# Feed-forward of a four-layer MetaFormer kernel: first product in one fp32 pass, two of three clips as a minimum on GpSimd

## The reference

```python
def quantize(y):                      # per group g of batch rows (here 5 groups)
    gamma = max(abs(y[g]))            # one number per group
    return clip(y[g] * 128 / (gamma + 1e-5), -128 + 1e-5, 128 - 1e-5)

def bitlinear(x, W, b):
    return quantize(x @ binarize(W).T + b)

h = gelu(bitlinear(layernorm(t), W1, b1))     # 96 -> 384
t = t + bitlinear(h, W2, b2)                  # 384 -> 96
```

## Time and profile before

| | |
|---|---|
| median of 3 runs | 970.29 us (969.41 to 970.37) |
| the profiled execution's own time | 968.89 us |
| its span | 967.0 us |
| busy: TensorE (PE) | 826.8 us, 86% |
| busy: VectorE (DVE) | 617.0 us, 64% |
| busy: GpSimd (POOL) | 560.8 us, 58% |
| busy: ScalarE (ACT) | 436.7 us, 45% |
| granted TensorE clock, mean | 0.918 |
| share of the chain that ended last, by engine | PE 63%, DVE 13%, POOL 8%, issue 8%, ACT 6% |

### The profile page before, as it was taken

The page is one execution under the profiler, slowest core; times in us unless marked ns, Lnnn a source line. Parts: engine busy times, 40 slices in busy tenths (PEclk is TensorE's granted clock), DMA queues, the critical chain, the costliest instruction groups (busy, mean ns, idle before and its releaser), DMA issues.

```text
span 967.0 us, 24067 instructions
## 1 busy us (share of the span) xinstructions
PE 826.8 (86%) x8814; PEld 681.2 (70%) x8814; DVE 617.0 (64%) x1713; ACT 436.7 (45%) x788; POOL 560.8 (58%) x887
## 2 busy tenths in 40 slices
PE   4666767767888999997999899999758998999997
PEld 3555655656666788876887677788757887778886
DVE  5765678637775777673667347677635665476755
ACT  1433345325555444433877354344134554544441
POOL 5333263143433886875776266887615666767855
PEclk9887679669999999997999899999956999999999
DMA  8500010000002101100001000100000001001020
GB/s 177 102 21 0 1 41 1 1 0 2 0 25 66 51 27 38 37 2 1 1 0 43 25 26 26 51 24 27 2 1 1 1 1 50 26 27 50 24 75 18
DMA packets 39512, 26.40 MB, mean 27 GB/s; under 512 B 27464, under 2 KB 32313, under 8 KB 39377
## 3 DMA queue, kind: packets, MB, share of 16 engines
q1 hardware_dynamic: 38428, 24.46, 10.1%
q10 hardware_dynamic: 998, 0.80, 0.3%
HBM read 8.33 MB, written 1.57 MB: 10 GB/s over the span
## 4 chain that ended last, share of the span: by engine, by line
PE 63%; DVE 13%; POOL 8%; issue 8%; ACT 6%; DMA 1%; ACTq 0%; POOLq 0%; DVEq 0%
PE PS L1522 17%; PE PS L1495 7%; PE PS L1496 6%; PE PS L1499 4%; PE PS L1438 3%; PE PS L1581 3%; PE PS L1593 2%; PE PS L1310 2%; ACT H L606 2%; PE PS L1622 2%; PE PS L1603 2%; PE PS L1296 2%; PE PS L1612 2%; PE PS L1357 1%; POOL H L514 1%
## 5 line engine op out<-in xcount | busy, mean ns | idle before, releaser
L648 ACT ACTIVATE H<-PS,B 128x512 f32<-128x512 f32 x288 | 176.9, 685 | 212.1 <-PE PS L1499 211.5
L1522 PE MATMUL PS<-M,H 128*64 128x96 f32 x4608 | 203.8, 249 | 7.2 <-DVE X L1134 7.2
L1522 PEld LDWEIGHTS PS<-M,H 128*64 128x64 f32 x4608 | 194.9, 139 | 18.2 <-DVE X L1134 7.8
L443 POOL TENSOR_TENSOR msum<-stats 128x4 f32<-128x4 f32 (+1 forms) x61 | 15.9, 260 | 277.4 <-DVE stats L808 240.4
L1134 DVE SCALAR_TENSOR_TENSOR X<-PS,G,X 128x96 f32<-128x96 f32 (+1 forms) x384 | 121.0, 317 | 66.3 <-PE PS L1522 55.8
L1496 PE MATMUL PS<-FHL,M1l 128*128 128x512 f32 x192 | 76.7, 400 | 0.0
L1495 PE MATMUL PS<-XH,M1h 128*128 128x512 f32 x192 | 76.6, 399 | 0.0
L487 POOL TENSOR_TENSOR ex<-euler,dl 128x16 f32<-128x16 f32 x24 | 69.8, 2910 | 8.6 <-DVE dl L1098 8.4
L479 POOL TENSOR_TENSOR PF<-G,B 128x1536 f32<-128x1536 f32 x24 | 66.2, 2756 | 10.0 <-DVE G L1125 10.0
L457 POOL TENSOR_TENSOR rs<-ve,half 128x4 f32<-128x4 f32 (+1 forms) x61 | 65.7, 1077 | 4.8
L1310 PE MATMUL PS<-ident,XN 128*96 128x128 f32 x224 | 39.1, 302 | 23.2 <-DMA WM<-L_conv_b_out 12.4
(11 more groups left out here) (250 smaller groups left out, 1928.3 us busy)
## 6 DMA issues: line engine op xcount, KB each, us to landing
FHL<-XH SPq DMA_DIRECT2D x36, 192.0 KB, 2.5
FHL<-XL SPq DMA_DIRECT2D x36, 64.0 KB, 2.2
X<-XH SPq DMA_DIRECT2D x12, 192.0 KB, 2.5
raw<-L_ffn_w SPq DMA_DIRECT2D x3, 576.0 KB, 4.7
M<-L_ffn_w SPq DMA_DIRECT2D x3, 576.0 KB, 6.0
X<-x SPq DMA_DIRECT2D x4, 384.0 KB, 6.2
XH<-XL SPq DMA_DIRECT2D x24, 64.0 KB, 1.9
out<-X SPq DMA_DIRECT2D x8, 192.0 KB, 2.4
```

The source lines that it names most:

```text
L648: act.activation(H[p][:, c, :], bank(UB[c]), ACT.Gelu, bias=B1[e][:, c:c + 1]).then_inc(gelu_a, 1)
L1522: ins = pe.matmul(Y[rows, x * C:(x + 1) * C], H[p][:, j, t * P + rows.start:t * P + rows.stop], M2[e][:, j, :], start=c == 0, stop=c == CH ...
```

## The change

The first product takes the transposed tokens in plain fp32 (tile FN in a free part of H) and is one fp32 matmul over 96 rows instead of two fp32r matmuls over 128; `ffn_lo` is gone, and so are the clearing of FH and FL. VectorE clips chunk 0 alone. Chunks 1 and 2 go unclipped through the gelu, behind which GpSimd takes the minimum with 128 - 1e-5, in place. ScalarE computes chunks 1, 2, 0 in this order. `down(q)` waits for GpSimd as well. GpSimd's order becomes normalise 0, normalise 1, minima of 0, normalise 2, minima of 1, normalise 3, minima of 2, normalise 4, minima of 3, minima of 4.

```diff
-        W1B = sb("W1B", [P, HID], F32R)
+        W1B = sb("W1B", [P, HID])
-        FH, FL = FHL[:, 0:FT * P], FHL[:, FT * P:2 * FT * P]
+        FN = hflat[0][:, 2880:2880 + FT * P]
@@ gpsimd
             attention(0, 0)
+            def ffn_prep(q):
+                normalise(q, EPS_T, FT, fst_v, fag_p, X[:, q * FT * C:(q + 1) * FT * C], FX, ft_pe, fxn_p)
+            def ffn_clip(q):
+                for c in range(1, CH):
+                    pool.wait_ge(ge_a, 3 * q + c)
+                    pool.tensor_scalar(YH[:, c, :], YH[:, c, :], QCLIP, None, ALU.min).then_inc(cl_p, 1)
+            ffn_prep(0)
+            ffn_prep(1)
             for q in range(FG):
-                normalise(q, EPS_T, FT, fst_v, fag_p, X[:, q * FT * C:(q + 1) * FT * C], FX, ft_pe, fxn_p)
+                ffn_clip(q)
+                if q + 2 < FG:
+                    ffn_prep(q + 2)
@@ scalar
             def ffn_hi(q):
                 act.wait_ge(ft_pe, q + 1)
-                act.activation(FH[0:C, :].rearrange(...), PS[...], ACT.Copy)
+                act.activation(FN[0:C, :].rearrange(...), PS[...], ACT.Copy)
...
-                    for c in range(CH):
-                        act.wait_ge(cl_v, 3 * (q + 1) + c + 1)
+                    act.wait_ge(qs1_v, 3 * (q + 1) + 3)
+                    for c in (1, 2, 0):
+                        if c == 0:
+                            act.wait_ge(cl_v, q + 2)
                         after(act, fd_pe, 2 * (q + 1))
                         act.activation(YH[:, c, :], Y1[(q + 1) % 2][:, c, :], ACT.Gelu, scale=qs[:, 0:1]).then_inc(ge_a, 1)
@@ vector
-            def ffn_lo(q):
-                ...
                         if g == 6:
-                            ffn_lo(0)
                             ffn_stats(1)
                             expert_weights(0)
...
-            dve.memset(FH[C:P].bitcast(F32), 0.0)
-            dve.memset(FL[C:P].bitcast(F32), 0.0)
...
-                    for c in range(CH):
-                        y = Y1[(q + 1) % 2][:, c, :]
-                        dve.tensor_scalar(y, y, ql[:, 0, 0:1], ql[:, 0, 1:2], ALU.min, ALU.max).then_inc(cl_v, 1)
-                if q + 2 < FG:
-                    ffn_lo(q + 2)
+                    y = Y1[(q + 1) % 2][:, 0, :]
+                    dve.tensor_scalar(y, y, ql[:, 0, 0:1], ql[:, 0, 1:2], ALU.min, ALU.max).then_inc(cl_v, 1)
@@ tensor
             def ffn_turn(q):
                 pe.wait_ge(fxn_p, q + 1)
-                after(pe, fl_v, q)
+                after(pe, fh_a, q)
...
                 if j == 0:
-                    pe.wait_ge(fl_v, q + 1)
+                    pe.wait_ge(fh_a, q + 1)
                 after(pe, y1_a, 6 * q + j - 2)
-                w, us = W1B[:, c * P:(c + 1) * P], slice(u * 3 * P, (u + 1) * 3 * P)
-                pe.matmul(bank(j % 3, 3 * P), w, FH[:, us], start=True, stop=False)
-                pe.matmul(bank(j % 3, 3 * P), w, FL[:, us], start=False, stop=True).then_inc(fu_pe, 1)
+                w, us = W1B[0:C, c * P:(c + 1) * P], slice(u * 3 * P, (u + 1) * 3 * P)
+                pe.matmul(bank(j % 3, 3 * P), w, FN[0:C, us], start=True, stop=True).then_inc(fu_pe, 1)
...
                 if 0 <= q < FG:
                     pe.wait_ge(ge_a, 3 * q + 3)
+                    pe.wait_ge(cl_p, 2 * q + 2)
                     after(pe, y2_v, 3 * q)
                     down(0, 2)
```

More of the change, by code:

```diff
@@ L243, in program @@
         fst_v, fag_p, fxn_p = (sem(n) for n in ("fst_v", "fag_p", "fxn_p"))
-        cl_v, ge_a, fd_pe, y2_v = (sem(n) for n in ("cl_v", "ge_a", "fd_pe", "y2_v"))
+        cl_v, cl_p, ge_a, fd_pe, y2_v = (sem(n) for n in ("cl_v", "cl_p", "ge_a", "fd_pe", "y2_v"))
         up_pe, gelu_a, dn_pe, gate_v, gexp_p, comb_v = (
@@ L576, in ffn_hi @@
                 act.wait_ge(ft_pe, q + 1)
-                act.activation(FH[0:C, :].rearrange("p (u n) -> p u n", u=2), PS[0:C, FT_BANKS[min(q, 1)], 0:3 * P], ACT.Copy)\
+                act.activation(FN[0:C, :].rearrange("p (u n) -> p u n", u=2), PS[0:C, FT_BANKS[min(q, 1)], 0:3 * P], ACT.Copy)\
                    .then_inc(fh_a, 1)
@@ L965, in _ @@
                .then_inc(wt_v, 1)
-            dve.memset(W1B[:].bitcast(F32), 0.0)
+            dve.memset(W1B[:], 0.0)
             dve.memset(W2B[:], 0.0).then_inc(wt_v, 1)
```

## The result

| | before | after |
|---|---|---|
| median | 970.12 us (969.41 to 970.37, 4 runs) | 986.27 us (983.92 to 987.46, 4 runs) |
| profiled execution, its span | 968.89, 967.0 us | 987.46, 985.6 us |
| ratio to before | | 1.0165 [1.0145, 1.0184] |

The change makes the kernel 16.15 us slower. The forecast was 985 us, within 973 to 990.

A forecast was written before the change was run, and what follows sets the result against it. Before, a feed-forward turn of 12.6 us without GpSimd bounds the stretch; the change closes a 19.0 us loop through GpSimd. 14.65 + 0.3 = 14.95 on 970.29 gives 985.2, say 985 us; range 973 to 990.

The forecast's parts named there:

- the closed loop: Feed-forward: second product, gelu of chunk 1, two minima, normalise, transposes, L1468, next second product; 19.0 us against 12.6 to 13.1.
- its three passes: Normalise 2, 3 and 4 each stand behind minima, so the second product of group 2 ends 14.65 us later.
- Head: Start of the feed-forward: without `ffn_lo(0)` the first gelus start at 128.2 in place of 132.44, 4.2 us won.
- The minimum: GpSimd minimum of 128x768 in the loop: 0.95 us each, 1.9 for two and 0.2 for handovers; bounds 0.87 and 1.5.
- Normalise: GpSimd's normalise in the loop: 6.3 us, against 6.53 before, since VectorE has fewer clips beside it; range 6.0 to 6.6.
- The transposes with L1468: Six transposes and L1468 ahead of each second product in the loop: 1.5 + 0.3 us, at half clock.
- The clock in the second product: Each second product in the loop starts at half clock, full clock returning 6.8 us into it: 7.8 us.
- Rival B: The loop at full clock: 15.2 us a turn, +3.25 + 0.3, about 974 us; chance 0.22.
- The sixth piece: Sixth fp32 up product of a group: +0.3 us, paid by group 4 only, otherwise idle time in the loop.
- `down`'s new wait: Second product waiting for GpSimd's minima in groups 3 and 4: no cost, or 0.1 us with minima at 1.5.
- the prediction's lower price: Lower bound for one GpSimd minimum in the loop: 0.87 us, memset rate plus 0.2; moves the forecast by -0.5 us.

The follow-up runs named there:

- Kernel 6: Kernel 2 plus seven single GpSimd instructions on unused space behind the last normalise (memset, minima, multiplication, two-operand product, minimum with maximum); 964.72 us, one execution.
- Kernel 4: The changed kernel plus 14 unread matmuls ahead of the transposes of groups 2, 3 and 4, where TensorE stands idle; 977.61 us, ratio 1.0070.
- kernel 5: The changed kernel with each GpSimd minimum over 384 of the 768 columns only; 977.83 us, ratio 1.0070.
- Kernel 7: The changed kernel with the minimum written as minimum and maximum in one instruction, the maximum changing nothing; 970.56 us, ratio 1.0007.
- kernel 2: The kernel before with the one-pass fp32 product alone, its three clips staying on VectorE; 968.29 us, ratio 0.9967.
- kernel 1: The changed kernel with GpSimd's order alone turned, normalise of group q+2 ahead of the minima of group q; 969.09 us, ratio 0.9983.

## Why the prediction was right, and where it was wrong

The mechanism was right at each step: the closed loop, its three passes, GpSimd's queue as the wait in front of the transposes, half clock in the second products. That the sum, 14.95 us against 16.15, came out so near is partly luck: errors of both signs met. Term by term, in the profiled execution with the 2.2 us taken off:

- **Head: right.** First gelus forecast at 128.2, measured 130.54 - 2.2 = 128.3. The transposes were released by L918 as forecast, and took 0.86 in place of 1.49.
- **The minimum: mis-sized.** The prediction took 0.95 each, with 0.87 and 1.5 as its ends; each took 2.13, outside both. I had put it near the memset "since it has one input". Kernel 6 shows that the number of inputs doesn't decide it: the one-input, one-operation form (2.12 to 2.14) takes longer than the two-input product (2.01). With the gelu and the handovers the three passes took 6.7 more than the terms forecast. The price that the prediction gave beside it by the Trainium skill (GPSIMD Engine Reference, Engine selection), 2.7 for the pair by its factor of two, is too low as well, against 4.23 measured. That page states the factor for two inputs; its "1-input is roughly line-rate" fits the 0.83 of the two-operation form (VectorE's is 0.67) and not the 2.13.
- **Normalise: 6.3 forecast**, 5.62, 5.85 and 5.83 measured up to the start of the transposes: 1.6 less over three passes. The transposes with L1468 were 0.8 less in sum, since L1468 overlaps the product.
- **The clock in the second product: about right in sum, not in each.** Forecast 7.8 in every turn. Measured 8.6, 5.6, 8.2: 1.0 less in sum. The moment at which full clock returned moved from turn to turn, so a turn was 18.3 us once and 20.9 once, for 19.0 forecast. Rival B, the loop at full clock, was forecast at 15.2 a turn. Kernel 4 shows that loop at 16.6: with the minima's real price (+2.3) and normalise's (-0.5) B's terms give 17.0.
- So the first three second products ended 18.0 later, for 14.65 forecast: 0.1 + 6.7 - 1.6 - 0.8 - 1.0 = 3.4, which is what lacked.
- **The sixth piece: +0.3 forecast**, 0.3 measured (8.16 between the second products of groups 2 and 3, 7.87 before). The product takes 0.71 from one to the next, 0.65 to 0.74 forecast.
- **`down`'s new wait: costed at nothing, or 0.1.** The second product of group 4 waited 2.69 us for L544 and started 5.4 after the one before it ended, not 4.1: 1.3 lost. It follows from the same mis-sized term; even the upper bound of 1.5 had left it at 0.1. Against it stood a second product of group 3 that was partly at full clock (7.4 for 8.7) and one of group 4 that was 0.6 shorter. The sum behind group 2 is -0.2, for +0.3.

So with minima as cheap as forecast the loss would have been smaller than forecast, and kernel 5 is the test of that: its pair took 2.31. Its second product of group 2 ended at 184.8, for 185.2 forecast, and its turns took 18.9 us each, for 19.0. The loop was forecast right for that price. What made this kernel's whole time lie 7 us below the forecast came later: 25.6 us from there to the end of the last second product, for 28.2 before (part of it at full clock, and no wait for GpSimd), 1.6 won back in the attention behind it, where the changed kernel won 1.4, and 2.0 in the phases behind that. None of these stood in the prediction, which let everything after group 2 shift as a whole.

Kernel 7 tests the lower end. Its pair of 1.64 lies just under the 1.74 of the prediction's lower price (0.87 each), for which its terms give 0.5 us less than the forecast, some 984.7. Measured were 970.56. The normalise and the wait were there; half clock in every turn was not: its three second products took 5.5, 4.8 and 7.8 us. The clock term of 7.8 thus held, roughly, in the changed kernel and in kernel 5, and not over the whole range of prices that the prediction had it cover.

**Left open.** Why full clock returned about 2 us into one second product of the loop (group 1), near the end of another (group 2) and not within the first isn't settled, nor what the attention behind the feed-forward wins back. In the profile of kernel 2 the second products end 3.0 to 3.8 us earlier than before, by the same correction of 2.2, while its median is lower by 1.9: within its interval, and not traced further. The gelu order 1, 2, 0 was never tried by itself.

## What to carry to other kernels

Before work is moved to an idle engine, draw that engine's queue as a line of waits: a step that waits for late data holds up the early step behind it, and if the late data depends on that early step a loop closes over all engines. Here the order of two lines was worth 17 us and the moved work itself gained nothing that shows. Look then at what the new gap does to TensorE's clock, which was about half of the loss, and at gaps that were there already: a few unread products in them were worth 6 to 9 us.

## What was not expected of the hardware

- On GpSimd a one-operation TENSOR_SCALAR in fp32 over 128x768 takes 2.12 to 2.14 us (minimum) and 2.50 (multiplication, one instruction, with VectorE busy beside it), and a minimum and maximum in one 0.83. Over 384 the minimum takes 1.16. A second operation that does nothing makes the minimum 2.6 times faster. Other pairs of operations weren't tried.
- With TensorE's idle gaps shortened from about 5 to 2.8, 2.2 and 2.2 us (kernel 7) the second product behind the second gap ran at full clock, with no unread work at all; the first came back to it midway, and the third ran at 0.56. Behind kernel 5's gaps of 3.6, 3.2 and 2.1 us the second products stayed at half clock, at 8.3 to 8.6 us each.
- The same kernel on the same chip moved by 13.7 us from run to run (kernel 1: 959.65 us at a mean granted clock of 0.939, 973.32 at 0.916). Differences of 1 to 2 us between such kernels can't be read from one profile each.
